# Two gather tables stored bucket by bucket, near diagonals walked down the rows, and all late query spreads on ACT

## The reference, cut to what matters

```python
c2p = jnp.einsum('bhqd,hpd->bhqp', q, pos_k)
c2p = jnp.take_along_axis(c2p, clip(rel + SPAN, 0, 2 * SPAN - 1), axis=-1) / scale
p2c = jnp.einsum('bhkd,hpd->bhkp', k, pos_q)
p2c = jnp.take_along_axis(p2c, clip(-rel + SPAN, 0, 2 * SPAN - 1), axis=-1)
scores = scores + c2p + swapaxes(p2c) / scale
```

## Time and profile before

| | |
|---|---|
| median of three runs | 2131.01 us (2130.97 to 2136.27) |
| the profiled execution | 2135.48 us, of which the span is 2133.7 us |
| bias stage, first spread to last DMA landed | about 979 to 1255 us |
| DVE busy | 1143.7 us (54%) |
| PE busy | 1485.9 us (70%) |
| ACT busy | 560.4 us (26%) |
| POOL busy | 715.1 us (34%) |

### The profile page before, as it was taken

One profiled execution on the slowest core, in us unless ns is written; L12 is line 12 of the kernel. 1 busy time (PEld: TensorE's weight loads), 2 busy tenths in 40 slices (PEclk: granted clock), 3 DMA queues, 4 the chain that ended last, 5 costly groups with the idle time before them and its releaser, 6 DMA issues. The chain is left out here.

```text
span 2133.7 us, 38821 instructions
## 1 busy us (share of the span) xinstructions
PE 1485.9 (70%) x13394; PEld 1261.3 (59%) x13394; DVE 1143.7 (54%) x3452; ACT 560.4 (26%) x1358; POOL 715.1 (34%) x829
## 2 busy tenths in 40 slices
PE   0699686985799963646844526999853588999840
PEld 0699564764588862525744414777742477888720
DVE  8951444338233325533499963777446655565534
ACT  0000232110144330102533313666321033333310
POOL 6420000005133328814647711111110633333256
PEclk9999998995599996767976657999855599999965
DMA  0000001000299973431144466555000089999943
GB/s 26 1 1 1 15 0 41 20 13 0 79 341 317 311 235 78 125 95 52 43 180 180 180 241 189 160 171 163 3 21 29 15 291 301 319 330 303 296 127 110
DMA packets 147184, 288.43 MB, mean 135 GB/s; under 512 B 33144, under 2 KB 114484, under 8 KB 145012
## 3 DMA queue, kind: packets, MB, share of 16 engines
q1 hardware_dynamic: 122356, 250.82, 34.7%
q0 software_dynamic: 24704, 35.93, 6.1%
HBM read 216.17 MB, written 70.35 MB: 134 GB/s over the span
## 5 line engine op out<-in xcount | busy, mean ns | idle before, releaser
L1741 PE MATMUL bi_ps<-bi_pos,bi_spread 64*32 64x128 f32 x4128 | 155.3, 314 | 98.5 <-POOL bi_spread L1723 49.9
L1723 POOL TENSOR_SCALAR bi_spread<-bi_rows,bi_hm 128x96 f32<-128x96 f32 x172 | 164.6, 981 | 139.1 <-PE bi_ps L1741 77.2
L1199 PE MATMUL ex_pg<-ex_xT,ex_w 128*128 128x128 f32 x1280 | 178.9, 283 | 46.3 <-DMA ex_w<-in_m_w 31.4
L1741 PEld LDWEIGHTS bi_ps<-bi_pos,bi_spread 64*32 64x32 f32 x4128 | 137.4, 126 | 116.5 <-POOL bi_spread L1723 61.6
L1170 POOL DMA_INDIRECT ex_xg<-moe_rows,ex_idx x160 | 155.9, 975 | 127.4 <-POOL ex_idx L1167 127.4
L1199 PEld LDWEIGHTS ex_pg<-ex_xT,ex_w 128*128 128x128 f32 x1280 | 157.4, 193 | 64.5 <-ACT ex_xT L1233 29.4
L334 PE MATMUL s_ps<-s_x,s_q 64*64 64x32 f32 x1024 | 129.9, 311 | 73.3 <-DVEq L286 73.3
L334 PEld LDWEIGHTS s_ps<-s_x,s_q 64*64 64x64 f32 x1024 | 129.7, 222 | 73.3 <-DVEq L286 73.3
L1199 PE MATMUL ex_pl<-ex_xT,ex_w 128*128 128x128 f32 x1280 | 172.3, 278 | 0.0
L1208 PE MATMUL ex_py<-ex_w,ex_mid 128*128 128x256 f32 x640 | 166.0, 382 | 1.0 <-DVE ex_mid L1297 0.6
L1199 PEld LDWEIGHTS ex_pl<-ex_xT,ex_w 128*128 128x128 f32 x1280 | 159.1, 195 | 0.0
(11 more groups left out here) (347 smaller groups left out, 2911.9 us busy)
## 6 DMA issues: line engine op xcount, KB each, us to landing
ex_w<-in_m_w SPq DMA_DIRECT2D x160, 771.0 KB, 5.8
a_bt<-attn_bias SPq DMA_DIRECT2D x64, 516.0 KB, 5.8
attn_bias<-bi_T SPq DMA_DIRECT2D x14, 2322.0 KB, 8.5
moe_y<-ex_y SPq DMA_DIRECT2D x160, 128.0 KB, 5.6
ex_xg<-moe_rows,ex_idx POOLq DMA_INDIRECT x160, 5.8
attn_v<-pj_v SPq DMA_DIRECT2D x8, 274.1 KB
a_v<-attn_v SPq DMA_DIRECT2D x8, 272.0 KB, 7.1
moe_rows<-mi_tn SPq DMA_DIRECT2D x17, 128.0 KB, 1.7
```

The lines of the kernel that those rows point to most:

```text
L1199: last = nc.tensor.matmul(banks[q][:, 0, f * P:(f + 1) * P], up(r, c, f0 + f), xT[q][:, c], start=c == 0, stop=c == KC - 1)
L1723: last = nc.gpsimd.tensor_scalar(dst, src, hm[:, hl:hl + 1], 1.0, ALU.mult, ALU.mult)
L1741: last = nc.tensor.matmul(ps[s % 4][g * MB:(g + 1) * MB, i // 3, (i % 3) * NBK:(i % 3 + 1) * NBK], spread[s % 2][rw, c, i], pos[rw, table, ...
```

## The change

Both tables are stored with the bucket as the outer and the token as the inner dimension. The C and D operands of all DVE additions and the target of ACT's copy follow from that. In single-bucket diagonals (L == 1) the order of the loops is exchanged: the buckets are now the outer and the rows the inner loop. POOL no longer spreads in the second half; ACT makes all four spreads of a late step. The number of instructions and of elements on DVE is as it was.

```diff
-        Dt = sb("Dt", [P, SP, NBK])
-        Ct = [sb(f"Ct{q}", [P, CMAX, NBK]) for q in range(2)]
+        Dt = sb("Dt", [P, NBK, SP])
+        Ct = [sb(f"Ct{q}", [P, NBK, CMAX]) for q in range(2)]
...
-            for s in range(2 * NS):
+            for s in range(NS):
                 spread_inputs(pool, s)
...
-                pe.wait_ge(spread_p, s + 1)
                 if s < NS:
+                    pe.wait_ge(spread_p, s + 1)
                     pe.wait_ge(spread_v, s + 1)
...
-                for hl in range(2, HH):
+                for hl in range(HH):
                     dst, src = spread_views(s, hl)
                     last = nc.scalar.activation(dst, src, ACT.Copy, scale=hm[:, hl:hl + 1])
...
-                nc.scalar.activation(target(s).rearrange("p (g i) n -> p g (i n)", g=2),
-                                     ps[s % 4][:, :, 0:BR // 2 * NBK], ACT.Copy).then_inc(out_ready, 1)
+                nc.scalar.activation(target(s).rearrange("p n (g i) -> p n g i", g=2),
+                                     ps[s % 4][:, :, 0:BR // 2 * NBK].rearrange("p g (i n) -> p n g i", n=NBK),
+                                     ACT.Copy).then_inc(out_ready, 1)
...
-                to, ci, di = (lo - i0) * SP + lo - d1, (lo - i0) * NBK + k, (lo - d1) * NBK + k
+                to, ci, di = (lo - i0) * SP + lo - d1, k * CMAX + lo - i0, k * SP + lo - d1
                 if L == 1:
-                    tv, cv, dv = ([SP + 1, m], [-1, count]), ([NBK, m], [1, count]), ([NBK, m], [1 - NBK, count])
+                    tv, cv, dv = ([-1, count], [SP + 1, m]), ([CMAX, count], [1, m]), ([SP - 1, count], [1, m])
                 else:
                     tv = [-L, count], [SP + 1, m], [-1, L]
-                    cv = [1, count], [NBK, m], [0, L]
-                    dv = [1 - L * NBK, count], [NBK, m], [-NBK, L]
+                    cv = [CMAX, count], [1, m], [0, L]
+                    dv = [SP - L, count], [1, m], [-1, L]
...
-                        V.tensor_tensor(rect[:, :, j0:j1], Cc[:, 0:n, k:k + 1].to_broadcast([P, n, j1 - j0]),
-                                        Dt[:, j0:j1, k].unsqueeze(1).to_broadcast([P, n, j1 - j0]), ALU.add).then_inc(t_far, 1)
+                        V.tensor_tensor(rect[:, :, j0:j1], Cc[:, k, 0:n].unsqueeze(2).to_broadcast([P, n, j1 - j0]),
+                                        Dt[:, k, j0:j1].unsqueeze(1).to_broadcast([P, n, j1 - j0]), ALU.add).then_inc(t_far, 1)
```

More of the change, by code:

```diff
@@ L1682, in target @@
             if s < NS:
-                return Dt[:, r0:r0 + BR]
+                return Dt[:, :, r0:r0 + BR]
             c = r0 // CMAX
-            return Ct[c % 2][:, r0 - c * CMAX:r0 - c * CMAX + BR]
+            return Ct[c % 2][:, :, r0 - c * CMAX:r0 - c * CMAX + BR]
         def table_copy(copy, s):
```

## The result

The changed kernel takes 2074.7 us (median of four runs, 2070.55 to 2077.95) against 2131.0 in the same comparison, 0.973 of the time before, 95% interval 0.970 to 0.976. Its profiled span is 2076.1 us, 57.6 less than before.

A forecast was written before the change was run, and what follows sets the result against it. DVE was taken to bound the bias stage's second half; -41.7 us of DVE time, +2 for the first chunk and +1 for the store made -39, from 2131 to 2092 us. The 8-in-10 range was 2077 to 2115.

The forecast's parts named there:

- Rectangles: DVE's 16 rectangles, second half of the bias stage: contiguous operands at 1.04 ns an element, 35.8 to 21.7 us, -14.1.
- Bands of L >= 2: DVE's 322 multi-diagonal instructions, second half: 32,234 elements at 1.35 ns, 80.4 to 66.1 us, -14.3.
- Near band: DVE's single-bucket band of 69 diagonals, 12 instructions: one jumping operand exchanged for another, still 1.78 ns an element, 0 us.
- Single diagonals: DVE's 450 one-diagonal instructions: C and D jumps go, T's stay, 2.1 to 1.78 ns on 4,190 elements, -1.3 us.
- POOL: POOL leaving the second half saves DVE 15 ns on each of 800 instructions, -12 us.
- The first chunk: Second half: ACT, now making four spreads and a copy a step, delays only DVE's first chunk, +2 us.
- ACT's copy: ACT's copy from PSUM at 128-word steps rises from 813 to about 890 ns; in the first half hidden behind PE, 0.
- The store: The store of T lands 8.3 us after issue, at most 9.1; DVE waits in the shortest chunks, +1 us.
- the signs that the prediction named for its own failure: In the new profile: ACT's copy passing 1.5 us, or the 1242-element band on DVE passing 3 us.
- Rival A: Bands and diagonals on DVE all near 1.04 ns, store holding chunks at about 9 us: -54, 2077 us; chance 0.14.
- B: DVE: jumps cost wherever they are, bands of L >= 2 at 1.75 ns, 69-diagonal band 2.2: -18, 2113 us; chance 0.17.

The follow-up runs named there:

- the probe: The changed kernel with 116 DVE additions of distinct sizes behind the last store, pricing one operand's jumps at a time; run once, only its profile counts.

## Why the prediction was wrong

The direction, the bound and the mechanism were right, and the size was not: 39 us forecast, 56 measured. On the profiled spans it is 57.6. By the prediction's steps:

1. Rectangles: -14.1 forecast, 35.8 to 22.4 = -13.4 measured. Nearly right, 0.7 us too much; the price read off the row held (1.03 ns).
2. Bands of L >= 2: this step failed. It took 1.35 ns an element, and they run at 1.04 to 1.10. On 32,234 elements this is 8 to 10 us; by the starts in the trace, which leave out the overlap of records, both L = 2 and L = 3 are at 1.04, and it is 10. The bounds were right; the choice between them was not. The L = 2 row (1.47 ns) was taken as nearest because its T has the shortest runs, though the prediction itself says that it held T's cost and D's jumps together; so it was only a ceiling for T. The step down to 1.35 left 0.31 ns for T's jumps between runs. Measured, they cost 0 to 0.06, and the probe shows that D's jumps with rereads alone bring 1.04 to 1.27.
3. Near band: 0 forecast, 2376 ns before and 2410 after. Right, and so is the reason: T's jump alone costs 1.76. Of the two figures that the Trainium skill has for a jumping destination (Vector Engine (DVE) Microarchitecture Reference, 5.2), the 1.71 agrees with this; steps of 24 words gave 2.22 here against its 2.50.
4. Single diagonals: failed in the same way. 1.78 was assumed, and one of 17 starts every 0.09 us, 70 + 1.04 n: T's slow writing hides under the next instruction's fixed time. 4,190 elements at 0.74 ns less are 3 us.
5. POOL: -12 forecast; 11.7 in the old layout and 12.9 in the new one. The sum was right, in part by luck: the two shapes from which the 15 ns were taken (17 and 37 ns dearer beside POOL, by a short window) were 9 and 12 ns dearer in the whole stage (268 against 259, 791 against 779), and the cost is some 70 interruptions of 0.17 us and not 15 ns everywhere. What was missed is the late C that a held-up POOL spread had caused, 3.6 us of DVE waiting, part of the 13.8 that the prediction put down to the first chunk nearly as a whole.
6. The first chunk: +2 forecast, nothing measured in this pair of profiles (71.8 us from the first matmul to DVE's first rectangle before, 71.4 after; 73 to 74 in two later profiles of the changed kernel). DVE's wait ahead of it is 10.2 us in both.
7. ACT's copy: 890 ns forecast, 841 and 825 measured, hidden as said. The spread stayed at 466 ns.
8. The store: +1 forecast, 0.7 us.

The errors add: 8 to 10 (step 2), 3 (4), 3.6 (5), 2 (6) and 0.3 (8) make 17 to 19 us, and the profiles lack 18.6 (57.6 less 39); the 0.7 us of step 1 goes the other way. So the large ones were on one side: in steps 2 and 4 the price had been taken between its ends, and the lower end came true. By the signs that the prediction named for its own failure, the copy and the 1242-element band, nothing was amiss; neither of them watched the step that failed.

Rival A gave 2077 us, nearly the time measured, but by luck: it wanted all bands at 1.04 and the store in control of the chunks. The near band stayed at 1.76, DVE needed 138 us and not 128, and the store held it 0.7 us in all. A's mechanism is real, as the run without the near band shows, but one step further on. B (jumps cost wherever they are) fell: its bands of L >= 2 at 1.75 ran at 1.04 to 1.10, and its near band at 2.2 stayed at 1.8.

## What to carry to other kernels

Where both inputs and the output of an addition jump, price each operand by itself before choosing an order: in the long additions here a jump of 128 words or more at each element cost 0.7 ns an element on T or on D, so exchanging one jumping operand for another bought nothing, and taking all of them away bought 40% (1.77 to 1.03 ns in the rectangles). A row in which two causes act together is a ceiling for each of them, not an estimate of either. An idle engine's small share of the bound engine's inputs can cost the bound engine more than it saves: POOL's 86 late spreads cost DVE 12 us and once made a chunk 3.6 us late. And once elements run at full rate, count instructions: 232 fewer were worth 14 us of DVE's time and 12 us of the whole.

## What the runs showed of the hardware that was not expected

- A jumping output costs 1.75 ns an element in back-to-back additions of 136 elements or more; up to 68 it is hidden, and one starts every 70 + 1.04 n ns. Jumping inputs are not hidden: 18-row diagonals, whose output jumps in both layouts, started every 107 ns before, when C and D jumped too, against 88 after.
- An input's jumps are cheaper when its words are read again three elements later (1.27 ns) and not when four later (1.69).
- An output in runs of 2 or 3 words, backwards, with a jump after each, runs at 1.10 and 1.04 ns; an input in runs of 18, half of them at odd starts, at 1.04.
- ACT reads PSUM in steps of 128 words across two banks for 841 instead of 813 ns per 768 elements.
- A POOL spread beside DVE's additions costs DVE 0.14 to 0.15 us in the mean, in both layouts, as some 70 interruptions of 0.17 us. It takes POOL itself 0.56 us when DVE is mostly idle, and 1.0 to 1.5 us here in the mean; but the median of the late ones is 0.56 us in the kernel before, and a few take up to 9.2.
